# Graph network with layer norm on one core: the root of the variance moves from GpSimd to VectorE, in batches

## What is computed

```python
width = CUTOFF / NUM_RBF * 0.5
rbf = jnp.exp(-(distances[:, None] - centers) ** 2 / (2.0 * width * width))
cut = 0.5 * (jnp.cos(jnp.pi * distances / CUTOFF) + 1.0) * (distances <= CUTOFF)
W = (jax.nn.silu(rbf @ fw1 + fb1) @ fw2 + fb2) * cut[:, None]
messages = (h[src] @ pw + pb) * W
agg = jax.ops.segment_sum(messages, dst, num_segments=num_atoms)
h1 = h + (jax.nn.silu(agg @ mw1 + mb1) @ mw2 + mb2)
y = x + h1
out = (y - mean(y)) / sqrt(var(y) + 1e-5)      # over the 128 features, h is x
```

## Time and profile before

| | |
|---|---|
| time, median of 3 runs | 1214.91 us (1213.65 to 1217.35) |
| profiled execution: time, span | 1215.85 us, 1214.1 us |
| PE, DVE, ACT, POOL busy | 54%, 48%, 29%, 51% of the span |
| chain that ended last | "another core or an unknown queue" 33%, DVE 24%, PE 18%, issue 11%, ACT 9% |
| first gather of the main loop | 79.9 us |

### The profile page before, as it was taken

One profiled execution on the slowest core, in us unless ns is written; L12 is line 12 of the kernel. 1 busy time (PEld: TensorE's weight loads), 2 busy tenths in 40 slices (PEclk: granted clock), 3 DMA queues, 4 the chain that ended last, 5 costly groups with the idle time before them and its releaser, 6 DMA issues.

```text
span 1214.1 us, 12087 instructions
## 1 busy us (share of the span) xinstructions
PE 661.1 (54%) x3533; PEld 569.2 (47%) x3593; DVE 579.6 (48%) x2078; ACT 346.4 (29%) x485; POOL 617.6 (51%) x688
## 2 busy tenths in 40 slices
PE   3943820572855138337454545747556766655673
PEld 3833720461745027226343435636455655544562
DVE  5654920481964038248533533974264343324443
ACT  2941400330422023113222032402233334333332
POOL 2136777126275731733663626674456565655651
PEclk9976765695777558668775767778677877867786
DMA  4944242021114121202142212313132222331110
GB/s 161 317 126 128 55 129 54 16 69 45 46 49 114 52 74 26 76 24 65 49 125 76 61 33 70 88 46 95 56 84 72 70 74 73 90 81 54 46 50 33
DMA packets 56693, 92.63 MB, mean 76 GB/s; under 512 B 12901, under 2 KB 32038, under 8 KB 56618
## 3 DMA queue, kind: packets, MB, share of 16 engines
q1 hardware_dynamic: 37450, 52.08, 14.2%
q0 software_dynamic: 19168, 39.68, 12.9%
HBM read 75.34 MB, written 16.37 MB: 76 GB/s over the span
## 4 chain that ended last, share of the span: by engine, by line
another core or an unknown queue 33%; DVE 24%; PE 18%; issue 11%; ACT 9%; DMA 2%; DVEq 1%; POOL 0%; SPq 0%; ACTq 0%; POOLq 0%
PE ps_sum L728 5%; PE ps_w L719 5%; DVE agg L1090 5%; DVE pairs L908 4%; PE ps_h L710 3%; DVE message L1074 3%; ACT act_t L614 2%; DVE member L1068 2%; ACT L614 2%; ACT L609 2%; ACT square L606 1%; DVE move L906 1%; ACT rbf L609 1%; DVE moves_now L904 1%
## 5 line engine op out<-in xcount | busy, mean ns | idle before, releaser
L513 POOL DMA_INDIRECT gathered<-proj_rows,src_tab x564 | 556.1, 986 | 234.6 <-issue 165.0
L1074 DVE TENSOR_TENSOR message<-ps_w,gathered 128x512 f32<-128x512 f32 x141 | 97.5, 692 | 385.1 <-remote 237.7
L728 PE MATMUL ps_sum<-member,message 128*128 128x64 f32 x1128 | 188.2, 321 | 162.6 <-DVE message L1074 101.4
L728 PEld LDWEIGHTS ps_sum<-member,message 128*128 128x128 f32 x1128 | 178.4, 239 | 172.5 <-DVE message L1074 110.8
L719 PE MATMUL ps_w<-fw_sb,act_t 128*128 128x128 f32 x1128 | 192.9, 325 | 113.3 <-issue 73.3
L614 ACT ACTIVATE act_t<-ps_h 128x512 f32<-128x512 f32 x141 | 82.2, 596 | 573.1 <-remote 443.3
L1090 DVE TENSOR_TENSOR agg<-agg,ps_sum 128x64 f32 x564 | 122.7, 218 | 186.9 <-remote 128.5
L719 PEld LDWEIGHTS ps_w<-fw_sb,act_t 128*128 128x128 f32 x1128 | 194.5, 242 | 36.1 <-issue 21.4
L710 PE MATMUL ps_h<-rbf,fw_halves 128*128 128x256 f32 x564 | 190.0, 463 | 23.9 <-issue 18.6
L1068 DVE TENSOR_SCALAR member<-iota_f,dst_tab,cut_tab 128x64 f32<-128x64 f32 x564 | 177.0, 322 | 1.1 <-issue 0.7
L716 PEld LDWEIGHTS ps_w<-bias_rhs,one_lanes 128*128 128x128 bf16 x141 | 15.2, 108 | 318.1 <-ACT act_t L614 181.5
(11 more groups left out here) (146 smaller groups left out, 539.9 us busy)
## 6 DMA issues: line engine op xcount, KB each, us to landing
dist_bc<-tile_dist SPq DMA_DIRECT2D x70, 256.0 KB
x_ring<-in_x SPq DMA_DIRECT2D x48, 256.0 KB, 4.5
gathered<-proj_rows,src_tab POOLq DMA_INDIRECT x564
proj_rows<-x_ring SPq DMA_DIRECT2D x24, 256.0 KB, 4.6
out_nodes<-x_ring SPq DMA_DIRECT2D x24, 256.0 KB
pair_rows<-pairs SPq DMA_DIRECT2D x4, 640.0 KB
dist_in<-in_edge_weight SPq DMA_DIRECT2D x5, 312.5 KB
src_in<-in_src SPq DMA_DIRECT2D x5, 312.5 KB
```

The source lines that it names most:

```text
L513: nc.gpsimd.indirect_dma_start(out=gathered[:, slot, :], out_offset=None, in_=proj, in_offset=bass.IndirectOffsetOnAxis(ap=table[:, c:c + ...
L728: last = nc.tensor.matmul(ps_sum[m % 2][:, WINDOW * t:WINDOW * (t + 1)], message[:, m % 2, t * P:(t + 1) * P], member[:, m % 2, t, :], sta ...
L1074: V.tensor_tensor(message[:, n % 2, :], ps_w[n % 2][:, :], gathered[:, MACRO * slot:MACRO * (slot + 1), :].rearrange("p t f -> p (t f)"), ...
```

## The change

The reciprocal root of variance + eps leaves GpSimd. VectorE makes a first guess from the bits of the number, and improves it by two Newton steps, for up to four chunks in one batch. The batches are `ROOTS`; a batch is made at the macro `rooted(lo)[0]`, which is the last chunk's `NODE_AFTER` + 5: macros 63, 86, 104, 119, 133, 142, 144 and 146. ScalarE normalises the chunks of a batch at + 3, + 4, + 5, + 6 from there, SyncE stores one macro after each of these and loads the next chunk three macros after the store. GpSimd's `scale` and its waits are gone, and `minus_half` and `minus_mean` with them. A batch of n chunks is nine instructions on 128 x 4n elements, each of which waits for the one before.

```diff
+ROOTS = ((0, 4), (4, 8), (8, 12), (12, 16), (16, 20), (20, 23), (23, 24), (24, 25))
+BATCH_OF = [next(b for b, (lo, hi) in enumerate(ROOTS) if lo <= i < hi) for i in range(CHUNKS)]
...
+ROOT_MAGIC = 1595932665.0
+ROOT_STEPS = ((0.703952253 * 2.38924456, -0.703952253), (1.5, -0.5))
...
+def rooted(i):
+
+    lo, hi = ROOTS[BATCH_OF[i]]
+    return NODE_AFTER[hi - 1] + 5, i - lo
...
             def nodes(m):
-                for i, after in enumerate(NODE_AFTER):
-                    if m == after + 9:
+                for i in range(CHUNKS):
+                    at, place = rooted(i)
+                    if m == at + 4 + place:
                         store_out(i)
-                    if m == after + 12 and i + RING < CHUNKS:
+                    if m == at + 7 + place and i + RING < CHUNKS:
                         load_x_again(i + RING)
...
-            def scale(i):
-                pool.wait_ge(node_stats, i + 1)
-                step(nc.gpsimd.tensor_tensor(rstd[:, i % RING, :], var_eps[:, i % RING, :], minus_half[:, :], ALU.pow))
-                step(nc.gpsimd.tensor_tensor(shift[:, i % RING, :], minus_mean[:, i % RING, :], rstd[:, i % RING, :],
-                                             ALU.mult))
-                pool.sem_inc(node_scaled, 1)
-
-            def nodes(m):
-                for i, after in enumerate(NODE_AFTER):
-                    if m == after + 8:
-                        scale(i)
-
             for m in range(MACROS):
                 prepare(m)
-                nodes(m)
...
             def normalise(i):
-                act.wait_ge(node_scaled, i + 1)
+                act.wait_ge(node_scaled, BATCH_OF[i] + 1 if i < CHUNKS else len(ROOTS) + i - CHUNKS + 1)
...
                 for i, after in enumerate(NODE_AFTER):
-                    if m == after + 8:
+                    at, place = rooted(i)
+                    if m == at + 3 + place:
                         normalise(i)
...
+            def roots(first, chunks):
+                of = slice(first % RING, first % RING + chunks)
                 settle()
-                step(V.tensor_scalar(var_eps[:, i % RING, :], mean_var[:, :, 1], EPS, None, ALU.add))
-                done(V.tensor_scalar(minus_mean[:, i % RING, :], mean_var[:, :, 0], -1.0, None, ALU.mult))
-                dve.sem_inc(node_stats, 1)
+                done(V.tensor_scalar(var_eps[:, of, :], mean_var[:, of, :, 1], EPS, None, ALU.add))
+                done(V.tensor_scalar(root_i[:, of, :], var_i[:, of, :], -0.5, ROOT_MAGIC, ALU.mult, ALU.add))
+                for n, (a, b) in enumerate(ROOT_STEPS):
+                    done(V.tensor_tensor(root_sq[:, of, :], root[:, of, :], root[:, of, :], ALU.mult))
+                    done(V.scalar_tensor_tensor(out=root_sq[:, of, :], in0=root_sq[:, of, :], scalar=b,
+                                                in1=var_eps[:, of, :], op0=ALU.mult, op1=ALU.mult))
+                    done(V.scalar_tensor_tensor(out=rstd[:, of, :] if n else root[:, of, :], in0=root_sq[:, of, :],
+                                                scalar=a, in1=root[:, of, :], op0=ALU.add, op1=ALU.mult))
+                done(V.scalar_tensor_tensor(out=shift[:, of, :], in0=mean_var[:, of, :, 0], scalar=-1.0,
+                                            in1=rstd[:, of, :], op0=ALU.mult, op1=ALU.mult))
+                dve.sem_inc(node_scaled, 1)
 
             def nodes(m):
                 for i, after in enumerate(NODE_AFTER):
                     if m == after + 4:
                         residual(i)
                         statistics(i)
+                for lo, hi in ROOTS:
+                    if m == rooted(lo)[0]:
+                        roots(lo, hi - lo)
```

More of the change, by code:

```diff
@@ L205, in build @@
         stats = sb("stats", [P, CHUNK, 6])
-        mean_var = sb("mean_var", [P, CHUNK, 2])
+        mean_var = sb("mean_var", [P, RING, CHUNK, 2])
         var_eps = sb("var_eps", [P, RING, CHUNK])
-        minus_mean = sb("minus_mean", [P, RING, CHUNK])
-        minus_half = sb("minus_half", [P, CHUNK])
+        var_i = var_eps.bitcast(I32)
+        root = sb("root", [P, RING, CHUNK])
+        root_i = root.bitcast(I32)
+        root_sq = sb("root_sq", [P, RING, CHUNK])
         rstd = sb("rstd", [P, RING, CHUNK])
@@ L294, in build @@
         node_summed = sem("node_summed")
-        node_stats = sem("node_stats")
         node_scaled = sem("node_scaled")
@@ L485, in _ @@
             step(nc.gpsimd.memset(all_ones[:, :], 1.0))
-            step(nc.gpsimd.memset(minus_half[:, :], -0.5))
             step(nc.gpsimd.affine_select(out=upto[:, :], in_=all_ones[:, :], compare_op=ALU.is_ge, fill=0.0,
@@ L560, in _ @@
                                 main.gathered[m % SLOT_MACROS])
-            for m in range(MACROS, NODE_END + 4):
-                nodes(m)
             pool.wait_ge(outside_ready, 1)
@@ L575, in _ @@
                                             general.gathered[j])
-                for i in range(CHUNKS, 2 * CHUNKS):
-                    scale(i)
         @block.scalar
@@ L1106, in statistics @@
                 for t in range(CHUNK):
-                    step(V.bn_aggr(mean_var[:, t, :], stats[:, t, :]))
+                    step(V.bn_aggr(mean_var[:, i % RING, t, :], stats[:, t, :]))
+            def roots(first, chunks):
+                of = slice(first % RING, first % RING + chunks)
                 settle()
-                step(V.tensor_scalar(var_eps[:, i % RING, :], mean_var[:, :, 1], EPS, None, ALU.add))
-                done(V.tensor_scalar(minus_mean[:, i % RING, :], mean_var[:, :, 0], -1.0, None, ALU.mult))
-                dve.sem_inc(node_stats, 1)
+                done(V.tensor_scalar(var_eps[:, of, :], mean_var[:, of, :, 1], EPS, None, ALU.add))
[9 more added lines that the diff above has]
+                dve.sem_inc(node_scaled, 1)
             def nodes(m):
@@ L1209, in _ @@
                     statistics(i)
+                    roots(i, 1)
 DVE_GENERAL_STEPS = 57
```

## The result

The changed kernel takes 1274.1 us (median of 4 runs, 1267.2 to 1279.1); the kernel before took 1216.1 us in the same comparison. The ratio is 1.046, with a 95% interval of 1.038 to 1.054: slower by 4.6%. Forecast was slower, 1226 us, and the measured time lies outside the range of 1185 to 1256. Some executions of a kernel fall in a slower state, over 1.5% above its fastest, and every ratio here leaves them out, so that it can differ a little from the quotient of two medians.

What follows compares the result with a forecast made beforehand. GpSimd's gather issue bounds, its long runs holding TensorE, so removed waits move to later stops. Last message 1195.5 + 27.4 + 2 = 1224.9 span, plus 1.75 gives 1226.6, median 0.9 lower: 1226 us; range 1185 to 1256.

Steps and rivals of the forecast that it cites:

- what bounds: GpSimd must issue 564 gathers, 4.96 us a macro in plain runs; long runs hold TensorE, so GpSimd's idle is not spare.
- B: Rival: short gather runs let all messages through, so from macro 109 slots come in time; 1195 us, chance 0.25.
- C: Rival: TensorE's holding has nothing to do with gathers, so removing GpSimd's waits pays fully; about 950 us, chance 0.06.
- D: Rival: idle is only moved, GpSimd's sum of idle stays as it is; 1215 us, chance 0.12.
- the stops: GpSimd's long waits at each group for tables, row numbers or stored pairs; 223 us of node waits move into them.
- the batches: Eight VectorE batches of nine dependent instructions, 0.22 us each, 2.0 us a batch; net between 0 and +8 us, 0 taken.
- Up to macro 109: Walk from stop to stop from 364 us: macro 109's first gather at 949.5, before at about 949.
- three messages in a plain run, restart of 8 us: A plain gather run lets three messages through; after a run over 60 us TensorE needs 8 us to restart.
- The stretch with slots: After 949.5 the 16 slots rule: macros 109 to 119 until 1004, then 21 macros at 6.2 us until 1134.
- The end without gathers: After the last gather, the 15 messages left take 3.85 us each, from 1137.5 to 1195.5.
- The tail: Behind the last message: 27.4 us as before, plus 2 for one more chunk normalised and the last root's ninth instruction.
- Rival E: Worse: each of six plain gather runs lets only two messages through, 5 us each, +30; 1256 us, chance 0.15.

Runs made afterwards that it cites:

- experiment 3: Changed kernel plus GpSimd memset of 128x1024 after each macro's four gathers: 1013.7 us, 0.834; other sizes and spacings of the memset: 1009.8 to 1267.9 us.
- experiment 1: Changed kernel with GpSimd's 25 waits put back: 1.016; with memsets as long as the old arithmetic behind them: 1224.0 us, 1.005; memsets without waits: 1.042.

## Why the prediction was right and wrong

*Right: what bounds.* The reading that unexplained waits behind TensorE belong to back-to-back gathers held in all runs; so did its consequence, that GpSimd's idle time is not spare. Rivals B, C and D fell: in this order 1195, 950 and 1215 were off by 79, 324 and 59 us. C's rule is that of the Trainium skill, SBUF — State Buffer, section "Who interferes with whom": TensorE and ScalarE never wait on anyone. It does not describe what is seen here: a memset on GpSimd took 377 us of ScalarE's waits for TensorE down to 89. Whether a port has a part in it, no run shows.

What is late can be read from the trace, which also has the times of semaphore updates. These are four groups of products on TensorE in the kernel before, in the long run of gathers that ends at 436.90:

```profile
388.82 1.92 PE L719 MATMUL ps_w<-fw_sb,act_t 128*128 128x128 f32 x8
403.28 1.97 PE L728 MATMUL ps_sum<-member,message 128*128 128x64 f32 x8 [12.55 <-issue]
405.04 2.27 PE L710 MATMUL ps_h<-rbf,fw_halves 128*128 128x256 f32 x4
...
437.19 1.92 PE L719 MATMUL ps_w<-fw_sb,act_t 128*128 128x128 f32 x8
```

Their updates stand at 445.22, 445.32, 445.38 and 445.48, four within 0.26 us. A group takes 1.0 us or more, so these had been computed before, and what came late was the report, in the order of issue. At times TensorE also computed late: inside a group it issued single products 1.2 to 3.5 us apart, though it waited for nothing that the profile shows (25 such steps on record, 44 us in all, before; 25 and 61 us in the changed kernel; none with the pause of experiment 3). Below are such products in the run of macros 95 to 108, and the silu behind it; four updates came together there at 944.73 to 944.98.

```profile
876.99 1.92 PE L719 MATMUL ps_w<-fw_sb,act_t 128*128 128x128 f32 x8
...
913.23 0.26 PE L728 MATMUL ps_sum<-member,message 128*128 128x64 f32 x1 [2.54 <-issue]
916.03 0.26 PE L728 MATMUL ps_sum<-member,message 128*128 128x64 f32 x1 [2.54 <-issue]
...
944.75 1.09 ACT L613 ACTIVATE act_t<-ps_h 128x512 f32<-128x512 f32 x2 [65.96 <-remote]
```

It looks like a backlog that grows with the run. Behind plain runs of 34.7, 49.7, 68.5 and 73.5 us in the changed kernel the updates come free together 4.9, 6.7, 8.8 and 9.5 us after the end, though GpSimd issues nothing then, and the last packet of its queue ends at most 2.2 us after the run. What the prediction calls a restart of TensorE is the time in which this backlog goes away.

*Right: the stops.* Where a stop was put, one is. Stored pairs of group 2: 381 forecast, 377.6 seen. Its tables: 479.5, 478.7. Row number of group 3: 558.5, 562.4. Its pieces: 614, 619.9. Macro 80: 712, 722.9. Row number of group 4: 791, 803.8. Its pieces: 846.5, 861.8. Macro 109: 949.5, 974.3.

*Right: the batches.* 0.20 us from one instruction to the next, 1.81 us for nine, where 0.22 and 2.0 were taken; and hardly a cost inside (with waits and arithmetic put back, experiment 1, the kernel is within 0.8% of before).

```profile
1250.17 0.17 DVE L1112 TENSOR_SCALAR var_eps<-mean_var 128x12 f32<-128x12 f32 x1
...
1251.81 0.17 DVE L1120 SCALAR_TENSOR_TENSOR shift<-mean_var,rstd 128x12 f32<-128x12 f32 x1
```

*Wrong: four terms of the sum.* The span came out at 1268.9 and not 1224.9, 44.0 us more:
- Up to macro 109, +24.8. From the tables of group 2 on each step to the next stop is 2 to 5 us longer than forecast, and the last one 9.5. It is the term "three messages in a plain run, restart of 8 us": in the run from 865.5 to 935.3 message 93 came at 866.1 and 94 at 897.9, and then nothing until 944.9, 9.6 us after the end; the sum had 95 inside the run.
- The stretch with slots, +16.3: from 974.3 to 1175.1 are 200.8 us, and 184.5 were taken. After the long run of ten macros the first two stops took 7.6 and 11.1 us, where 3.4 + 0.9 was the price of every stop; from macro 119 on it is 6.5 us a macro (1031.6 to 1175.1, 22 macros) instead of 6.2.
- The end without gathers, +7.3: 68.8 us from the last gather to the last message against 61.5. 15 macros took 4.5 us each (1177.0 to 1243.9) and not 3.85. Part of this is a slip: 231.93 to 267.31 are the starts of macros 13 and 22, nine macros apart and not ten, so 3.9 us each and not 3.54, and the mean with 4.15 is 4.04, which is 2.9 us more for 15. A likely cause of the rest, which no run tests, is the node work: in the last 16 macros six chunks fall due.
- The tail, -4.4: 25.0 us behind the last message, with the batches, where 27.4 + 2 was taken.

The step that failed is thus the size of the hold in a plain run of gathers: three messages let through, and then 8, 5 or 3.4 us of standing. In five of the six plain runs the message that the walk had as the last inside (39, 47, 75, 95, 103) came only behind the end, and the first message behind it came 5.0 to 12.5 us after the end. These are the first two terms, 41 of the 44 us, but for the little that a plain run's pace adds, 5.00 us a macro instead of 4.96. The price of a run over 60 us stood on a single run, 371.27 to 436.90 with 8.3 us behind it; the three of over 65 us in the changed kernel took 8.3, 12.5 and 9.6. Rival E had the right mechanism, one message less per run, with a chance of 0.15, and its 1256 was still 18 short of the median. The forecast's own range (35 us) was read as if the doubts of eight stops were independent; seven of the eight steps erred the same way. The forecast of "slower" had 0.52 and was for 10 us of the 58: the mechanism was right, its size was not.

*Wrong: what removing arithmetic is worth.* I counted the 32 us of root and product as gone without asking what they had been good for. Beside the waits they are worth 1.2% in experiment 1, and the memsets of experiment 3 say it more plainly: a busy GpSimd that issues no gather also lets TensorE through.

## What to carry to other kernels

Idle or foreign work on an engine that issues gathers can be what keeps the others going; before such a wait is removed, look at what the other engines do in it. A wait that nobody ended and that recurs in step with another engine's bursts is best tested by slowing that engine: here a pause of 1 us per macro made the kernel 17% faster than before. And a lead of 16 macros is not better than one of 4 if the producer's lead costs the consumer (0.853 with 4 in the same ring).

## What the runs showed of the hardware

TensorE's results reach ScalarE and VectorE late while GpSimd issues indirect gathers at its full rate, one each 1.25 us (0.94 and a gap of 0.30). Signals from VectorE and ScalarE to TensorE are not late: in the traces of before and after, where TensorE had stood over 1.5 us for a silu or a message, its next weight load began 0.05 us after the end of that (95 cases). It does not hang on bytes (64 or 512 a row), and it fades as the gathers are spaced: of 947 us of waits that nobody ended 903 are left at 1.33 us a gather, 546 at 1.43, 250 at 1.49, 12 at 1.51 and none at 1.55. The cause inside the chip is not shown by any run. All times here are of executions that the profiler recorded; whether TensorE reports as late in one that it does not record is not shown either.

The fastest kernel run is the changed one with 128x512 after every two gathers, 1009.8 us, 0.841 (0.836 to 0.847) of the kernel before; the one with 128x1024 after four is level with it (1013.7 us; 0.834, 0.829 to 0.839, in its own comparison). Of the waits in the first, those of VectorE for gathers on their way are now the largest that bear on the messages, 265 us.
